# Value products of windowed attention over eight array tiles, in a fused adaLN kernel (Mamba block and transformer)

## The reference

```python
x = L0_attn_resid                       # (2, 1024, 128)
h = _layernorm(x) * (1 + ca) + sa
x = x + ga * mamba(h)                   # a selective scan over 1024 positions
h = _layernorm(x) * (1 + cb) + sb
for i in range(6):                      # the transformer, _L0_ffn_ref
    h = attn_layer(shift_tokens(h), Wqkv[i], ...) + h
    h = ffn_layer(shift_tokens(h), ...) + h
x = x + gb * h
```

```python
sim = einsum('bhwie,bhwje->bhwij', bq, bk2) * 8      # 32 queries x 64 keys
sim = where(mask, -big, sim)
attn = softmax(sim, -1)
out = einsum('bhwij,bhwje->bhwie', attn, bv2)        # 32 queries x 64
```

## Time and profile before

| | us |
|---|---|
| median of 3 runs | 2239.24 |
| lowest, highest | 2236.26, 2240.97 |
| the profiled execution, its own time | 2243.84 |
| its span, first to last instruction | 2242.0 |

### The profile page before, as it was taken

One profiled execution on the slowest core, in us unless ns is written; L12 is line 12 of the kernel. 1 busy time (PEld: TensorE's weight loads), 2 busy tenths in 40 slices (PEclk: granted clock), 3 DMA queues, 4 the chain that ended last, 5 costly groups with the idle time before them and its releaser, 6 DMA issues. The chain is left out here.

```text
span 2242.0 us, 85216 instructions
## 1 busy us (share of the span) xinstructions
PE 2071.2 (92%) x32996; PEld 1482.2 (66%) x32996; DVE 1628.2 (73%) x3071; ACT 1472.3 (66%) x4549; POOL 1239.9 (55%) x1377
## 2 busy tenths in 40 slices
PE   7788888999899999899998999999999989999997
PEld 3332335885775976866857758768768678597672
DVE  1498897985775966867857759668678577596673
ACT  4522225976775967867767759668678667596772
POOL 1465865764753754754647536548546465375450
PEclk9888789999999999999999999999999999999998
DMA  1311112111121211211111212112211111111010
GB/s 57 133 66 66 65 38 78 41 39 33 41 74 29 50 37 34 75 44 37 39 34 38 77 28 50 35 36 49 70 37 41 34 35 42 28 50 30 24 29 19
DMA packets 148103, 104.46 MB, mean 47 GB/s; under 512 B 15778, under 2 KB 140256, under 8 KB 146176
## 3 DMA queue, kind: packets, MB, share of 16 engines
q1 hardware_dynamic: 147712, 99.07, 15.9%
HBM read 48.31 MB, written 1.18 MB: 22 GB/s over the span
## 5 line engine op out<-in xcount | busy, mean ns | idle before, releaser
L1371 POOL TENSOR_TENSOR QK<-PC,PS 128x256 f32<-128x256 f32 x384 | 279.5, 728 | 604.6 <-DVE PS L1282 579.9
L1121 ACT ACTIVATE PR<-ps,MN 128x64 f32<-128x64 f32 x1536 | 356.1, 314 | 390.3 <-DVE MN L1243 390.2
L1376 POOL TENSOR_TENSOR QK<-QK,RN 128x512 f32<-128x512 f32 x384 | 402.0, 1047 | 158.4 <-ACT RN L1111 131.0
L995 PE MATMUL ps<-W,XS 128*128 128x256 f32 x1536 | 397.9, 382 | 4.1 <-PEq L64 4.1
L967 PE MATMUL ps<-V,PT 64*32 64x65 f32 x12288 | 301.3, 220 | 10.0 <-ACT PT L1162 5.0
L995 PEld LDWEIGHTS ps<-W,XS 128*128 128x128 f32 x1536 | 263.5, 192 | 25.0 <-issue 4.9
L1372 POOL TENSOR_TENSOR QK<-PC,PS 128x256 f32<-128x256 f32 x384 | 279.8, 729 | 0.0
L981 PE MATMUL ps<-ident,QK 128*128 128x128 f32 x1536 | 252.0, 287 | 29.3 <-POOL QK L1376 29.3
L967 PEld LDWEIGHTS ps<-V,PT 64*32 64x32 f32 x12288 | 256.5, 105 | 18.5 <-ACT PT L1162 11.0
L1266 DVE TENSOR_REDUCE SS<-SQ 128x8 f32<-128x512 f32 x384 | 259.3, 675 | 4.6 <-ACT SQ L1153 4.4
L1243 DVE TENSOR_REDUCE MN<-ps 128x4 f32<-128x256 f32 x384 | 161.3, 420 | 138.4 <-PE ps L948 134.9
(11 more groups left out here) (138 smaller groups left out, 3461.7 us busy)
## 6 DMA issues: line engine op xcount, KB each, us to landing
V<-V SPq DMA_DIRECT2D x384, 97.5 KB, 2.2
scr<-B_rows SPq DMA_DIRECT2D x32, 512.0 KB, 3.7
V<-V SPq DMA_DIRECT2D x288, 32.5 KB, 2.0
W<-in_Wqkv SPq DMA_DIRECT2D x40, 192.0 KB, 2.8
TC<-in_tcos SPq DMA_DIRECT2D x6, 1024.0 KB, 5.0
TS<-in_tsin SPq DMA_DIRECT2D x6, 1024.0 KB, 8.3
WO<-in_Wo SPq DMA_DIRECT2D x6, 512.0 KB, 4.3
W<-in_W SPq DMA_DIRECT2D x6, 341.0 KB, 4.0
```

The source lines that it names most:

```text
L995: mm = nc.tensor.matmul(ps[:, par, k * 2 * P:(k + 1) * 2 * P], cols[k], W[:, i, 0:2, :].rearrange("p t m -> p (t m)"), start=True, stop=True)
L1121: e = nc.scalar.activation(PR[:, m % 2, h, slot * DH:(slot + 1) * DH], ps[:, 4 + h, slot * DH:(slot + 1) * DH], ACT.Exp, scale=-1.0, bias= ...
L1371: nc.gpsimd.tensor_tensor(QK[:, par, :, 0:hd], PC[:, par, :, 0:hd], PS[:, par, :, hd:DH], ALU.add)
L1376: nc.gpsimd.tensor_tensor(QK[:, par, :, :], QK[:, par, :, :], bcast_last(RN[:, par, :], DH), ALU.mult).then_inc(qk, 1)
```

## The change

`slot_quad` goes, and `window(slot, quad)` with a list of eight tiles comes. Values: the output quadrant is now the one in which the probabilities' columns stand, and the slot chooses the bank, 5 or 6, so that all eight pairs of row half and quadrant occur, each once for each head. v moves from bank 3 to bank 5, columns 256 to 511, the transposed probabilities to bank 6, same columns; scores and transposed outputs move down one bank, to 3 and 4. The scores' 16 products are issued slot by slot in the order of the tile list, which alternates between the row halves (heads). The waits follow the banks: `values` waits for `v_cp` at min(n, NSTEPS), which counts `copy_v` of the round before; v's product and `p_transposed` wait for `on` at n-6 (`normalise` of the same round); `copy_v` no longer waits for `pT_ps`. `normalise` reads two banks, and `copy_out` puts the windows back in order.

The diff:

```diff
@@ -912,8 +912,10 @@
             sp.wait_ge(w_1, 16 * DEPTH)
             sp.wait_ge(w_2, 32 * DEPTH)
-        def slot_quad(j):
-            return (j % 4) // 2, (j // 4) * 2 + j % 2
+        def window(slot, quad):
+            return quad // 2 * 4 + slot * 2 + quad % 2
+
+        spread_tiles = [(0, 0), (1, 2), (0, 1), (1, 3), (0, 2), (1, 0), (0, 3), (1, 1)]
         @block.tensor
         def _(pe):
@@ -926,7 +928,7 @@
                 pe.wait_ge(on, m + 1)
                 for k in range(2):
                     src = ON[:, m % 2, :, :].rearrange("p (k h) d -> p k (h d)", k=2)[:, k, :]
-                    mm = nc.tensor.transpose(ps[:, 4, (1 + k) * P:(2 + k) * P], src, ident[:])
+                    mm = nc.tensor.transpose(ps[:, 3, (1 + k) * P:(2 + k) * P], src, ident[:])
                 mm.then_inc(oT_ps, 1)
             def scores(n):
@@ -939,13 +941,12 @@
                 wait(pe, pr, m)
                 wait(pe, oT, m - 3)
                 for h in range(2):
-                    nc.tensor.matmul(ps[:, 4 + h, 0:P], identb[:], MASKB[:, int(s == 0), h, :], start=True, stop=True)
+                    nc.tensor.matmul(ps[:, 3 + h, 0:P], identb[:], MASKB[:, int(s == 0), h, :], start=True, stop=True)
                 pe.wait_ge(qkT, m + 1)
-                for h in range(2):
-                    for j in range(8):
-                        slot, quad = slot_quad(j)
-                        c0 = PAD + s * STEP + j * WIN
-                        mm = nc.tensor.matmul(ps[32 * quad:32 * quad + 32, 4 + h, slot * DH:(slot + 1) * DH],
+                for slot in range(2):
+                    for h, quad in spread_tiles:
+                        c0 = PAD + s * STEP + window(slot, quad) * WIN
+                        mm = nc.tensor.matmul(ps[32 * quad:32 * quad + 32, 3 + h, slot * DH:(slot + 1) * DH],
                                               QKT[DH * h:DH * h + DH, 0, c0:c0 + WIN],
                                               QKT[DH * h:DH * h + DH, 1, c0 - WIN:c0 + WIN],
                                               start=False, stop=True, skip_group_check=True)
@@ -958,13 +959,12 @@
                 pe.wait_ge(pT, m + 1)
                 pe.wait_ge(v_sh[m % 4], 32 * (m // 4 + 1))
                 wait(pe, on, m)
+                wait(pe, v_cp, min(n, NSTEPS))
                 for h in range(2):
-                    for j in (0, 2, 1, 3, 4, 6, 5, 7):
-                        slot, quad = slot_quad(j)
+                    for slot, quad in spread_tiles:
+                        j = window(slot, quad)
                         r = slice(64 * slot, 64 * slot + 64)
-                        q = j % 4
-                        g = (j // 4) * 2 + h
-                        mm = nc.tensor.matmul(ps[32 * q:32 * q + 32, 6, g * (DH + 1):(g + 1) * (DH + 1)],
+                        mm = nc.tensor.matmul(ps[32 * quad:32 * quad + 32, 5 + slot, h * (DH + 1):(h + 1) * (DH + 1)],
                                               PT[r, m % 2, h, 32 * quad:32 * quad + 32],
                                               V[r, 2 * (m % 8) + j // 4, 2 * (1 - j % 2) + h, :], start=True, stop=True)
                 mm.then_inc(o_ps, 1)
@@ -996,9 +996,9 @@
                                           W[:, i, 0:2, :].rearrange("p t m -> p (t m)"), start=True, stop=True)
                 mm.then_inc(qk_ps, 1)
                 wait(pe, v_cp, n)
-                wait(pe, pT, n - 6)
+                wait(pe, on, n - 6)
                 for k in range(2):
-                    mm = nc.tensor.matmul(ps[:, 3, k * P:(k + 1) * P], cols[k], W[:, i, 2, :], start=True, stop=True)
+                    mm = nc.tensor.matmul(ps[:, 5, (2 + k) * P:(3 + k) * P], cols[k], W[:, i, 2, :], start=True, stop=True)
                 mm.then_inc(v_ps, 1)
             def p_transposed(n):
@@ -1007,9 +1007,9 @@
                     return
                 pe.wait_ge(pr, m + 1)
                 wait(pe, pT, m)
-                wait(pe, v_cp, min(n, NSTEPS))
+                wait(pe, on, m)
                 for h in range(2):
-                    mm = nc.tensor.transpose(ps[:, 3, (2 + h) * P:(3 + h) * P], PR[:, m % 2, h, :], ident[:])
+                    mm = nc.tensor.transpose(ps[:, 6, (2 + h) * P:(3 + h) * P], PR[:, m % 2, h, :], ident[:])
                 mm.then_inc(pT_ps, 1)
             def out_proj(t, c):
@@ -1119,7 +1119,7 @@
                 for h in range(2):
                     for slot in range(2):
                         e = nc.scalar.activation(PR[:, m % 2, h, slot * DH:(slot + 1) * DH],
-                                                 ps[:, 4 + h, slot * DH:(slot + 1) * DH], ACT.Exp, scale=-1.0,
+                                                 ps[:, 3 + h, slot * DH:(slot + 1) * DH], ACT.Exp, scale=-1.0,
                                                  bias=MN[:, m % 2, 2 * h + slot:2 * h + slot + 1])
                 e.then_inc(pr, 1)
@@ -1133,7 +1133,8 @@
                 act.wait_ge(mn, min(n - 4, NSTEPS))
                 if i == 0 and m >= PHASE:
                     act.wait_ge(wo_ps, 2 * (m // PHASE - 1) + s // 2 + 1)
-                nc.scalar.copy(OT[:, s // 2, i, (s % 2) * STEP:(s % 2 + 1) * STEP], ps[:, 4, P:3 * P]).then_inc(oT, 1)
+                nc.scalar.copy(OT[:, s // 2, i, (s % 2) * STEP:(s % 2 + 1) * STEP].rearrange("p (w k c) -> p k w c", w=2, k=2),
+                               ps[:, 3, P:3 * P].rearrange("p (k w c) -> p k w c", k=2, w=2)).then_inc(oT, 1)
             def copy_qk(n):
                 m = n - 3
@@ -1159,7 +1160,7 @@
                     return
                 act.wait_ge(pT_ps, m + 1)
                 wait(act, o_ps, m - 1)
-                nc.scalar.copy(PT[:, m % 2, :, :].rearrange("p h q -> p (h q)"), ps[:, 3, 2 * P:4 * P]).then_inc(pT, 1)
+                nc.scalar.copy(PT[:, m % 2, :, :].rearrange("p h q -> p (h q)"), ps[:, 6, 2 * P:4 * P]).then_inc(pT, 1)
             def copy_v(n):
                 if n >= NSTEPS:
@@ -1167,11 +1168,10 @@
                 act.wait_ge(v_ps, n + 1)
                 if n < 6:
                     act.wait_ge(s_ones, 2)
-                wait(act, pT_ps, n - 5)
                 wait(act, o_ps, n - 7)
                 k0 = 2 * (n % 8)
                 nc.scalar.copy(V[:, k0:k0 + 2, 0:2, 0:DH],
-                               ps[:, 3, 0:2 * P].rearrange("p (k a d) -> p k a d", k=2, d=DH)).then_inc(v_cp, 1)
+                               ps[:, 5, 2 * P:4 * P].rearrange("p (k a d) -> p k a d", k=2, d=DH)).then_inc(v_cp, 1)
             def logs(n):
                 m = n - 1
@@ -1241,7 +1241,7 @@
                 dve.wait_ge(s_ps, m + 1)
                 wait(dve, pr, m - 1)
                 nc.vector.tensor_reduce(MN[:, m % 2, :].rearrange("p (h a) -> p h a", h=2),
-                                        ps[:, 4:6, 0:P].rearrange("p h (a d) -> p h a d", d=DH),
+                                        ps[:, 3:5, 0:P].rearrange("p h (a d) -> p h a d", d=DH),
                                         AX.X, ALU.min).then_inc(mn, 1)
             def normalise(n):
@@ -1249,13 +1249,14 @@
                 if not 0 <= m < NSTEPS:
                     return
                 dve.wait_ge(o_ps, m + 1)
-                o = ps[:, 6, 0:4 * (DH + 1)].rearrange("p (a d) -> p a d", d=DH + 1)
+                o = ps[:, 5:7, 0:2 * (DH + 1)].rearrange("p s (h d) -> p s h d", h=2)
+                inv = RC[:, m % 2, :].rearrange("p (s h) -> p s h", s=2)
                 wait(dve, on, m - 1)
-                nc.vector.reciprocal(RC[:, m % 2, :].unsqueeze(2), o[:, :, DH:DH + 1]).then_inc(rc, 1)
+                nc.vector.reciprocal(inv.unsqueeze(3), o[:, :, :, DH:DH + 1]).then_inc(rc, 1)
                 dve.wait_ge(rc, m + 1)
                 wait(dve, oT_ps, m - 1)
-                nc.vector.tensor_tensor(ON[:, m % 2, :, :], o[:, :, 0:DH], bcast_last(RC[:, m % 2, :], DH),
-                                        ALU.mult).then_inc(on, 1)
+                nc.vector.tensor_tensor(ON[:, m % 2, :, :].rearrange("p (s h) d -> p s h d", s=2), o[:, :, :, 0:DH],
+                                        bcast_last(inv, DH), ALU.mult).then_inc(on, 1)
             def norms(n):
                 m = n - 1
```

## The result

The change made the kernel slower: 2245.91 us in place of 2236.66 us (medians of 20 runs each, taken together), a ratio of 1.0037 with a 95% interval of 1.0028 to 1.0046. The forecast was 2200 us. One execution of a later variant, the kernel before without its small maximum, took 4549.86 us; no ratio counts it, and that variant's median is 2225.41 us with it and 2224.64 us without. The profiled execution of the changed kernel has a span of 2247.8 us, against 2242.0.

The account below looks back on a forecast made before the run. TensorE was taken to set the pace at 3.45 us per step; 348 steps x 0.08 = 28 and 36 x 0.33 = 12 made 40 us less, 2200 us against a median of 2239.24; range 2160 to 2246.

Parts of the forecast that it names:

- the burst: Value products on TensorE: eight tiles instead of four shrink the burst by some 0.20 us; qk_transposed follows 0.39 us after the first.
- the structure of two loops: Chains through V's copy: from p_transposed, 3.30 us per step; from the scores over two steps, 6.76 us, 3.38 per step.
- the moved banks: Scores and out_transposed: nothing; v and p_transposed wait for normalise, at most 0.1 us if VectorE runs late.
- the score order: Scores alternating over both row halves: at most 0.05 us of the 0.27 us burst, 0.02 per step.
- the added wait: values(n) also waits for V's copy; with 0.05 us handover the first value product starts 0.21 us later.
- The first loop: From p_transposed to V's end 1.06, handover 0.05, values to qk_transposed 0.39, to next p_transposed 1.80: 3.30 us per step.
- VectorE's bound: VectorE's own cycle: a free step of 2.93 us and a held one of 3.83 alternate to 3.38.
- Rival B: No net change: VectorE's late minimum falls on the loop; plain steps 3.43 to 3.45 us, total 2224 or 2240; 11%.
- Rival C: Slower: queue order, not tile count, spaces the products; values stay at 0.59 us, scores go to 0.44; 2281 us; 13%.
- rival A: The V wait costs less as ScalarE's chain tightens; plain steps fall to 3.23 us, total 2155 us; 12%.
- the 28 us of the plain steps: Gain forecast for 348 steps at 0.08 us each, a plain step going to 3.37 us.
- the 12 us at the block work: Gain forecast for 36 steps between two blocks of work, each keeping the full 0.33 us.

Follow-up runs that it names:

- the wait alone: Kernel before, with only one addition: values(n) also waits for v_cp at min(n, NSTEPS); 2277.99 us, ratio 1.0196.
- the half-by-half run: Changed kernel with each head's value products issued as four quadrants of row half 0, then four of half 1; 2248.24 us, one execution.
- both edits: Changed kernel without VectorE's small maximum (an added bias in ScalarE's logarithm instead) and with the v_cp wait on the weight load; 2189.11 us, ratio 0.9797.

## Why the prediction was wrong

Right were: TensorE's lead before; the burst (0.24 us forecast and measured) and qk_transposed 0.39 us after it; the wait for V as the new stop; the structure of two loops, one of them over two steps; no cost of the moved banks beyond the wait (ON at p_transposed is waited for only 4.1 us in all, and four tiles in the moved banks pace like the wait alone in the old ones); the score order as a small gain.

The step that failed first is the handover in **the added wait**: 0.05 us, from a row in which PT was the last to be met. There the wait for PT rides on the weight load. The wait for `v_cp` was put into the separate semaphore instruction, and the handover is 0.144 us. The first loop is then 1.07 + 0.14 + 0.39 + 1.80, 3.41 us with the thousandths, not 3.30, and longer than the second, which I had taken for the limit (3.38 in the prediction, and 3.37 with the dearer handover and the 3.754 us that ScalarE's part takes when nothing delays it: 6.736 by two). With the handover that I assumed, plain steps are indeed 3.32. The row priced another form of the same wait.

The step that failed second is **VectorE's bound**: "a free step of 2.93 and a held one of 3.83 alternate to 3.38". The rows had one free step followed by two held ones, and I made a pair of them. Three give 2.93 + 3.84 + 3.83, 3.53 per step. In the changed kernel's rows the free step is 2.86, and the three sum to 10.53 (1499.38 to 1509.91), 3.51 per step: the mean measured at both handovers, in the stretches of undisturbed cycles. It is not a fixed pace of VectorE, as pairs occur too: in the rounds 18 to 31 and 0 to 4 of the kernel before I find 36 such threes and 22 pairs of one free and one held step, in the changed kernel 45 and 4. Why the changed kernel settles on threes stays open. Lateness had been slack: before, the values did not depend on the V copy of the round, so a late minimum was caught up. Rival B has this mechanism with its place, but I gave it 11% and let VectorE catch up at 3.38; at 3.51 it does not.

By size: with the maximum gone, handover 0.144 gives 2214 us and handover 0.05 gives 2189. So the assumed handover is worth 25 us once nothing else stops it, and VectorE's maximum, hold and all, costs 32 us at the one and 49 at the other (2238.53 less 2189.11). With one of the two steps mended the other error would have stayed: 2238 with the cheap handover and VectorE's maximum, 2214 the other way round. Rival C, the order in the queue, is refuted by the burst of 0.24 us itself, and the half-by-half run agrees; rival A's 3.23 was not reached, not even with both edits (3.32).

Of the sum, the 28 us of the plain steps came as a loss of 10.8, and the 12 us at the block work came as 4.1. One term is a little off in itself: 0.33 us, from a stretch of 0.42, stands beside 0.39 for the same stretch, which gives 0.36 and 13 us for 12; it decides nothing.

The range, up to 2246.0, held the 2245.91 by 0.09 us. That is luck: its upper end was set by where the shares of rivals B and C were cut off, not by the steps that failed. The sign was wrong, and the chance of slower was 14%.

## What to carry to other kernels

A resource shared to save time brings a wait, and the wait's worth is read from the whole loop it closes: which copy it waits for, what that copy waits for, and over how many rounds. Before you price it, list every engine, and every round trip between two engines, whose own cycle is near the present step, over enough steps to see its pattern, since slack that absorbed a late step goes as soon as the step is on the loop. And where several waits stand before one instruction, let the one that is met last ride on the instruction itself: here its place in the source was worth 0.09 us per step, 25 us of 2214.

## What the runs showed of the hardware that was not expected

- A VectorE maximum over 8 elements per partition in SBUF, 0.17 us by itself, took 0.86 to 0.94 us in rows above and in the earlier trace rows, until GpSimd's two-operand multiplication ended, with two tensor operands and with one. In the changed kernel all 204 maxima that started with over 0.3 us of that multiplication to go ended with it, within 0.06 us. The reduction of 512 elements kept its 0.67 to 0.69 us in all 384 cases, 350 of them beside a GpSimd instruction.
- The last-met wait in a separate semaphore instruction of TensorE gave 0.144 us from the producer's end to the first product; on the weight load, 0.052 us.
- Sixteen fp32 products of 64x32 by 64x65 take 0.44 us from first to last start on four tiles, whether in one bank or two, and 0.25 us on eight, in either order.
